# First stage of a fused conditional-mix, state-space and table-FFN kernel: how code bits are cut out of words, the order of its loads and expert network, and where dt is transposed

## The chip, the cores and the metric

The kernel runs on one core of a Trainium2 chip. A core has TensorE (PE: products, and transposes by an identity, into PSUM), VectorE (DVE), ScalarE (ACT), GpSimd (POOL) and SyncE (SP), which here only issues DMAs. Each engine works through a queue of its own in order and waits on semaphores. The metric is device time in microseconds, lower is better.

## The reference

Cut to what matters here (x is 128 x 32 x 512, `cond_128` is 128 x 128):

```python
h = gelu(cond @ W0 + b0); h = gelu(h @ W1 + b1)
att = softmax(h @ W2 + b2)                      # 8 experts
agg_w = einsum('bk,koi->boi', att, weight)      # one 32x32 mix matrix per batch
hidden = einsum('boi,bih->boh', agg_w, x) + (att @ bias_k)[:, :, None]
proj = hidden @ in_proj_w.T                     # gate, conv channels, and dt: the last 64 columns
dt_p = softplus(dt + dt_bias)
x = x + attention_like_scan(proj, dt_p, ...)    # second stage of the kernel
y = conv(x) + (cond @ c_weight.T)[:, :, None] + bias
# dequantisation: bit p of a weight's code is a bit of int32 plane p, 32 positions a word
idx = sum(((qweight[p][:, :, None] >> arange(32)) & 1) << p)   # p < 4 or p < 8
w_low, w_high = lut4[o, idx4], lut8[o, idx8]
out = x + where(norm(y) > 64, y @ w_high.T, y @ w_low.T) + bias
```

## The kernel before, in words

The program has three stages, one behind the other; a block ends when all engines are through it. The change touches the first, `stage1`; it ends at about 182 of 3663 us. The second (projections, convolution, scan) takes nearly all of the rest.

`stage1` first loads 14 small tensors from SP, and TensorE waits for all of them. The expert network is a chain over TensorE, ScalarE and VectorE (L276 to L293, L342 to L348, L401 to L427) to `agg`, the mix matrices. SP writes `agg`, `aggb` and `ctxb` to memory and reads them back as block-diagonal `mix` and `aggb_row` (L203 to L211). Then comes a loop over eight blocks of 512 tokens, in pairs (u is 0 or 1). For a block, TensorE makes four chunks of the hidden state (`mix_chunk`, eight matrix passes and one bias product each), ScalarE copies a chunk's high part (L372), VectorE subtracts it for the low part (`low_part`, L474), SP stores both (`h_d`, 2 MB) and loads the next x. `dt_block` (L316) makes dt, ScalarE and VectorE make its softplus (L359 to L363, L455, L458). GpSimd copies x by phases (`xp`, L270).

VectorE also does the work of the third stage's weights. `take_bits` (L391) cuts the bits of 8 planes out of `qw`: a byte of a word, shifted by s % 8 and masked by 1, for 32 bit positions and two halves of planes, so 64 instructions of 128x256 bytes; 28 stand ahead of the logits (L409) and 36 behind `att_t` (L417). L435 to L440 make `mask0` and the high code. Inside the loop `pair` (L465) and `join` (L470) build low-bit weights from `mask0`, `low_bits` and `lut4`. Behind the loop dt is transposed for all eight blocks (L336) and copied to `dt_all` (L509), by two PSUM banks that `dt_block` used.

## Time and profile before

| | before |
|---|---|
| median of 3 runs (lowest, highest) | 3664.96 us (3662.59, 3664.98) |
| profiled execution: its time, its span | 3664.37 us, 3662.6 us |
| TensorE, VectorE, ScalarE, GpSimd busy in the span | 3521.4, 3122.5, 1453.2, 469.3 us |
| mean granted TensorE clock | 0.988 |
| first product over the tokens starts | 70.28 us |
| last VectorE instruction of the first stage ends | 182.20 us |

The span is from the first to the last instruction of the profiled execution; 1.8 us of its time lie around it. Rows of the timeline give a start, a length, and in brackets how long the engine was idle before it and what released it.

### The profile page before, as it was taken

To read this page: it belongs to the slowest core of one execution; us is meant where nothing else is said; L and a number is where in the kernel's file an instruction comes from. 1 tells how busy PE (TensorE), PEld (TensorE's weight loads), DVE (VectorE), ACT (ScalarE), POOL (GpSimd) and SP (SyncE) were. 2 spreads that over 40 slices of the span, in tenths; PEclk is the share of its full clock that TensorE was granted. 3 is DMA by queue.
4 is the path that set the end of the run, shared out by engine and by line. 5 is a ranking of instruction groups with operands and counts; after the bars stand their busy time and mean duration, and the time that the engine had idled before them with its cause. 6 is when DMAs were issued, how large, how long until landed. Compare 5 with 4: busy or idle time off the path is not lost. (4 is left out here: it accounts for less than half of the span.)

```text
span 3662.6 us, 58842 instructions
## 1 busy us (share of the span) xinstructions
PE 3521.4 (96%) x19789; PEld 2880.3 (79%) x19789; DVE 3122.5 (85%) x4932; ACT 1453.2 (40%) x2215; POOL 469.3 (13%) x297
## 2 busy tenths in 40 slices
PE   3779999999999999999999999999999999998999
PEld 2568888888888888888888888888888888886888
DVE  7769999999999999999999999999999999997343
ACT  1534444444444444444444444444444444443111
POOL 2200011111000111110011111001111110010333
PEclk9889999999999999999999999999999999998999
DMA  3733335333533244323632353234333353334331
GB/s 95 309 127 114 126 115 183 126 126 116 178 135 126 103 161 160 126 109 115 206 112 105 126 206 117 110 123 177 132 115 126 129 186 115 126 111 128 102 96 55
DMA packets 220670, 490.26 MB, mean 134 GB/s; under 512 B 39594, under 2 KB 85066, under 8 KB 211042
## 3 DMA queue, kind: packets, MB, share of 16 engines
q1 hardware_dynamic: 217060, 489.10, 38.0%
q0 software_dynamic: 304, 0.82, 0.1%
q10 hardware_dynamic: 3280, 0.04, 0.1%
q8 instruction: 11, 0.18, 0.0%
q14 instruction: 15, 0.12, 0.0%
HBM read 320.51 MB, written 169.39 MB: 134 GB/s over the span
## 5 line engine op out<-in xcount | busy, mean ns | idle before, releaser
L743 PE MATMUL bank<-ht,wt 128*128 128x512 f32 x7680 | 1862.9, 397 | 7.3 <-DMA ht<-h_d 7.3
L743 PEld LDWEIGHTS bank<-ht,wt 128*128 128x128 f32 x7680 | 1427.2, 188 | 352.8 <-issue 18.5
L965 DVE SCALAR_TENSOR_TENSOR xc<-bank,cvw,xc 128x496 f32<-128x496 f32 (+2 forms) x1152 | 821.0, 717 | 95.9 <-ACT xc L880 45.4
L880 ACT ACTIVATE xc<-bank,cvb,cvw 128x512 f32<-128x512 f32 x384 | 299.3, 779 | 1126.7 <-PE bank L743 1126.7
L838 PE MATMUL bank<-wot,gy 128*128 128x512 f32 x3072 | 737.5, 396 | 0.0
L838 PEld LDWEIGHTS bank<-wot,gy 128*128 128x128 f32 x3072 | 567.3, 188 | 127.5 <-issue 11.0
L719 POOL TENSOR_TENSOR r<-rv,neg_half 128x4 f32<-128x4 f32 x64 | 89.7, 1402 | 2490.5 <-DVE rv L1053 2490.5
L987 DVE TENSOR_TENSOR m<-cbm,y 128x1024 f32<-128x1024 f32 x256 | 301.5, 1220 | 7.8
L716 POOL TENSOR_TENSOR segr<-adts,mask_le 128x1024 fp32r<-128x1024 f32 x128 | 242.7, 1917 | 381.5 <-DVE adts L956 381.5
L870 ACT ACTIVATE gy<-z 128x512 fp32r<-128x512 f32 x256 | 162.0, 633 | 320.5 <-DVE z L1027 320.5
L866 ACT ACTIVATE z<-bank 128x512 f32<-128x512 f32 x256 | 150.6, 588 | 278.9 <-PE bank L743 278.9
L760 PE MATMUL bank<-m,dtx 128*64 128x128 f32 x4096 | 251.8, 276 | 0.0
L760 PEld LDWEIGHTS bank<-m,dtx 128*64 128x64 f32 x4096 | 220.9, 137 | 34.2 <-issue 34.2
L862 ACT ACTIVATE xc<-xc 128x512 f32<-128x512 f32 x384 | 233.2, 623 | 14.4 <-DVE xc L965 13.7
L1023 DVE SCALAR_TENSOR_TENSOR y<-xc,dsk,bank 128x512 f32<-128x512 f32 x256 | 190.1, 743 | 47.3 <-PE bank L760 47.3
L1027 DVE SCALAR_TENSOR_TENSOR z<-z,nw,y 128x512 f32<-128x512 f32 x256 | 192.3, 751 | 26.6
L1265 PE MATMUL p_y<-wq,x3t 128*128 128x512 f32 x768 | 189.1, 402 | 0.0
L994 DVE TENSOR_TENSOR dtx<-bank,dt_all 128x512 f32<-128x512 f32 x256 | 168.0, 689 | 21.6 <-PE bank L750 17.5
L1016 DVE TENSOR_TENSOR gy<-z,gy 128x512 fp32r<-128x512 f32 x256 | 175.4, 685 | 0.0
L1065 DVE SCALAR_TENSOR_TENSOR acc<-bank,r,acc 128x512 f32<-128x512 f32 x256 | 173.7, 742 | 0.0
L1265 PEld LDWEIGHTS p_y<-wq,x3t 128*128 128x128 f32 x768 | 143.4, 190 | 32.6
L933 DVE TENSOR_SCALAR leaf<-mask,lut 128x512 int32<-128x512 int32 x320 | 166.9, 538 | 0.0
(162 smaller groups left out, 3088.5 us busy)
## 6 DMA issues: line engine op xcount, KB each, us to landing
ht<-h_d SPq DMA_DIRECT2D x64, 2048.0 KB, 7.8
acc<-acc_d SPq DMA_DIRECT2D x64, 1024.0 KB, 7.2
wt_d<-wnext SPq DMA_DIRECT2D x128, 512.0 KB, 3.1
acc_d<-acc SPq DMA_DIRECT2D x64, 1024.0 KB, 4.3
wt<-wt_d SPq DMA_DIRECT2D x70, 512.0 KB, 8.2
stage<-in_L_attn_in_proj_w SPq DMA_DIRECT2D x106, 256.0 KB, 2.7
h_d<-ht_out SPq DMA_DIRECT2D x8, 2048.0 KB, 7.2
wot<-wt_d SPq DMA_DIRECT2D x28, 512.0 KB, 6.2
```

The costliest lines, as they stand in the source:

```text
L716: pool.tensor_tensor(segr[:, half, :, :], adts[:, half, :].bitcast(F32).unsqueeze(2).to_broadcast([P, TT * HG, L]), sh.mask_le[:, :].unsqu ...
L743: ins = pe.matmul(pb[:, :], wt[:, n, l, k, :], ht[:, rr, k, :], start=(q == 0 and k == 0), stop=(q == 2 and k == KC - 1))
L760: ins = pe.matmul(bank[YB[c % 2]][u * HP:(u + 1) * HP, t * P:(t + 1) * P], dtx[:, t, h * HP:(h + 1) * HP], m[:, h, t, :], start=True, stop ...
L838: ins = pe.matmul(bank[OUT[t]][:, :], gy[:, c, l, t * P:(t + 1) * P], wot[:, rr, c, :], start=(c == 0 and q == 0), stop=(c == CT - 1 and q ...
L862: act.activation(xc[:, n, :], xc[:, n, :], ACT.Silu).then_inc(s_silu, 1)
L880: act.activation(xc[:, n, :], bank[PROJ_BANK[n]][:, :], ACT.Identity, bias=cvb[:, n:n + 1], scale=cvw[:, n, TAPS - 1:TAPS]).then_inc(s_tap, 1)
L965: ins = dve.scalar_tensor_tensor(dst, src, cvw[:, n, TAPS - 1 - k:TAPS - k], dst, ALU.mult, ALU.add)
L987: dve.tensor_tensor(m[:, :, t, :].rearrange("p h (c l) -> p h c l", l=L), cbm[:, t, :].rearrange("p (c l) -> p c l", l=L).unsqueeze(1).to_ ...
L1016: dve.tensor_tensor(gy[:, c, 1, :], z[:, c, :], gy[:, c, 0, :].bitcast(F32), ALU.subtract).then_inc(s_ulo, 1)
L1023: dve.scalar_tensor_tensor(y[:, c, :], xc[:, 2 + c, :], dsk[:, c:c + 1], bank[YB[c % 2]][:, :], ALU.mult, ALU.add).then_inc(s_y, 1)
L1027: dve.scalar_tensor_tensor(z[:, c, :], z[:, c, :], nw[:, c:c + 1], y[:, c, :], ALU.mult, ALU.mult).then_inc(s_u, 1)
L1265: ins = pe.matmul(p_y[t % 2][q][:, :], x3t[:, l, t, r, :], wq[:, q, rr, r, :], start=(n == 0 and r == 0), stop=(n == 2 and r == R - 1))
```

## The change

Four edits, all in `stage1`:

- **Bits.** `bits` is [128, 8 planes, 4, 512] bytes. One instruction shifts whole int32 words of `qw` by s (0 to 7) and masks them by 0x01010101, so that each of the four bytes of a result is one bit of one plane. There are 8 instructions of 128x512 words, each writing every eighth word. The bytes then lie in another order than the positions. Three ScalarE copies of 2048 bytes put planes 1 to 3 in order (`low_bits`), the `mask0` instruction does it for plane 0 as it reads, and a ScalarE copy behind the loop does it for the high code. The high code is joined by shifts and ORs of words, in six instructions behind the loop. All bit work stands behind the expert network.
- **Loads.** Six small loads come from SP, ahead of x; four needed ones and four later ones come from ScalarE's queue. TensorE waits for the first ten only. GpSimd makes the identity first and issues the loads of `qw` and the tables after `mix` is cleared.
- **Expert network.** The transposes of `wdt` and their copies move to its end, so ScalarE's first function is Gelu. The side product goes to `p_h[0]`.
- **dt.** `turn_dt` transposes block 2jj-2 and 2jj-1 in the next pair's loop round, into the banks `p_mlp` and `p_wdt`, which the loop left unused; `keep_dt` copies on VectorE. Two blocks are left for the end. TensorE's loop is written out.

```diff
+        def by_position(plane):
+
+            return plane.rearrange("p t (w s k) -> p t w k s", s=8, k=4)
...
+                for dst, src in ((cond[:, :], a["cond_128"]), (w0[:, :], a["L0_cond_W0"]),
+                                 (b0[:, :], a["L0_cond_b0"].rearrange("(p o) -> p o", o=1)),
+                                 (w1[:, :], a["L0_cond_W1"]),
+                                 (b1[:, :], a["L0_cond_b1"].rearrange("(p o) -> p o", o=1)),
+                                 (w2[:, :], a["L0_cond_W2"])):
                     sp.dma_start(dst, src).then_inc(s_ld, 16)
-                sh.n_small = 16 * len(small)
...
-                pe.wait_ge(s_ld, sh.n_small)
-                pe.wait_ge(s_const, 4)
+                pe.wait_ge(s_ld, 16 * NLD)
+                pe.wait_ge(s_const, 2)
                 pe.transpose(p_mlp[:, 0:NB], cond[:, :], sh.ident[:, :])
                 pe.transpose(p_mlp[:, NB:NB + L], cw[:, :], sh.ident[0:L, 0:L]).then_inc(s_pe, 1)
+                pe.wait_ge(s_dve, 2)
+                pe.matmul(p_mlp[:, 256:256 + NB], w0[:, :], cond_t[:, :], start=True, stop=True).then_inc(s_pe, 1)
+                pe.matmul(p_h[0][:, 0:L], cond_t[:, :], cw_t[:, :], start=True, stop=True).then_inc(s_pe, 1)
+                pe.wait_ge(s_act, 1)
+                pe.matmul(p_mlp[:, 384:384 + NB], w1[:, :], h1[:, :], start=True, stop=True).then_inc(s_pe, 1)
+                pe.wait_ge(s_act, 2)
+                pe.matmul(p_mlp[:, 192:192 + NEXP], h2[:, :], w2[:, :], start=True, stop=True).then_inc(s_pe, 1)
...
+                pe.wait_ge(s_ld2, 16 * NLD2)
...
                 pe.wait_ge(s_mix, 16 * (BT + 1))
-                with pe.Fori(0, NBLK // 2) as jj:
+                pe.wait_ge(s_dve, 11)
+
+                def turn_dt(j, u):
+                    pe.wait_ge(s_dtsp, j + 2)
+                    pe.wait_ge(s_dt, j + 1)
+                    for t in range(TT):
+                        ins = pe.transpose(p_dtT[u][:, t * H:(t + 1) * H], dt_t[:, ds(j * BLK + t * P, P)], sh.ident[0:H, 0:H])
+                    ins.then_inc(s_dtT, 1)
+
+                def pair_of_blocks(jj, first):
...
                     dt_block(0)
+                    if not first:
+                        turn_dt(2 * jj - 2, 0)
                     mix_chunk(1, 2)
                     mix_chunk(1, 3)
                     dt_block(1)
...
-                pe.wait_ge(s_dtpos, NBLK + 2)
-                for j in range(NBLK):
-                    pe.wait_ge(s_dtsp, j + 2)
...
+                    if not first:
+                        turn_dt(2 * jj - 1, 1)
+
+                pair_of_blocks(0, True)
+                for jj in range(1, NBLK // 2):
+                    pair_of_blocks(jj, False)
+                turn_dt(NBLK - 2, 0)
+                turn_dt(NBLK - 1, 1)
...
+                for dst, src in ((cw[:, :], a["L0_cond2_c_weight"]), (b2[:, :], a["L0_cond_b2"].partition_broadcast(NB)),
...
+                                 (bias_k[:, :], a["L0_cond_bias_k"])):
+                    act.dma_start(dst, src).then_inc(s_ld, 16)
+                for dst, src in ((side[:, :], a["fside_S_0"].partition_broadcast(NB)),
...
+                                 (alog[:, :], a["L0_attn_A_log"].partition_broadcast(P))):
+                    act.dma_start(dst, src).then_inc(s_ld2, 16)
                 act.wait_ge(s_pe, 2)
+                act.activation(h1[:, :], p_mlp[:, 256:256 + NB], ACT.Gelu, bias=b0[:, :]).then_inc(s_act, 1)
+                act.wait_ge(s_pe, 4)
+                act.activation(h2[:, :], p_mlp[:, 384:384 + NB], ACT.Gelu, bias=b1[:, :]).then_inc(s_act, 1)
+                act.wait_ge(s_dve, 4)
+                act.activation(att[:, :], logit[:, :], ACT.Exp, bias=nmax[:, :], accum_out=esum[:, :]).then_inc(s_act, 1)
+                act.wait_ge(s_pe, 8)
...
+                act.wait_ge(s_bits, 1)
+                for b in (1, 2, 3):
+                    act.activation(sh.low_bits[:, b, :, :].rearrange("p t (w k s) -> p t w k s", s=8, k=4), by_position(bits[:, b, :, :]),
+                                   ACT.Copy).then_inc(s_plane, 1)
                 high_pair(0, True)
                 with act.Fori(1, NBLK // 2) as jj:
                     high_pair(jj, False)
                 softplus_log(NBLK - 1, 1)
+                act.wait_ge(s_bits, 6)
+                act.activation(sh.hi[:, :, :].rearrange("p t (w k s) -> p t w k s", s=8, k=4), by_position(bits[:, 4, :, :]),
+                               ACT.Copy).then_inc(s_plane, 1)
...
-                def take_bits(first, last):
-
-                    for half, planes in enumerate((sh.low_bits, high_bits)):
-                        for s in range(first, last):
-                            ins = dve.tensor_scalar(planes[:, :, :, :].rearrange("p n t (w s) -> p n t w s", s=32)[:, :, :, :, s],
-                                                    qbyte[:, 4 * half:4 * half + 4, :, :, s // 8], s % 8, 1,
-                                                    ALU.logical_shift_right, ALU.bitwise_and)
+                bit_words = bits[:, :, :, :].rearrange("p n t i -> p (n t i)").bitcast(I32)
+                WORDS = OT * DM // 4
+
+                def take_bits():
+
+                    v = bit_words.rearrange("p (n t w s) -> p n t w s", n=8, t=OT, s=8)
+                    for s in range(8):
+                        ins = dve.tensor_scalar(v[:, :, :, :, s], qw[:, :, :, :].rearrange("p t n w -> p n t w"), s,
+                                                byte_ones[:, :].bitcast(I32), ALU.logical_shift_right, ALU.bitwise_and)
                     ins.then_inc(s_bits, 1)
...
-                dve.wait_ge(s_q, 16 * (OT + 2))
-                take_bits(0, 14)
+                dve.wait_ge(s_pe, 5)
+                dve.tensor_tensor(logit[:, :], p_mlp[:, 192:192 + NEXP], b2[:, :], ALU.add).then_inc(s_dve, 1)
...
-                dve.tensor_scalar(att[:, :], att[:, :], erec[:, :], None, ALU.mult).then_inc(s_dve, 1)
+                dve.tensor_copy(att_t[:, :], p_agg[0][0:NEXP, 0:NB]).then_inc(s_dve, 1)
+                dve.wait_ge(s_ld2, 16 * NLD2)
                 dve.wait_ge(s_pe, 7)
-                dve.tensor_copy(att_t[:, :], p_agg[0][0:NEXP, 0:NB]).then_inc(s_dve, 1)
-                take_bits(14, 32)
-                dve.wait_ge(s_pe, 8)
...
+                dve.wait_ge(s_act, 4)
+                dve.tensor_tensor(wdt_t[:, 1, :, :].rearrange("p k h -> p (k h)"), p_wdt[:, 0:KC * H],
+                                  wdt_t[:, 0, :, :].rearrange("p k h -> p (k h)").bitcast(F32), ALU.subtract).then_inc(s_dve, 1)
...
+                dve.wait_ge(s_q, 16 * (OT + 2))
...
-                dve.tensor_scalar(sh.mask0[:, :, :], sh.low_bits[:, 0, :, :], -1.0, None, ALU.mult).then_inc(s_bits, 1)
-                dve.scalar_tensor_tensor(hi_sum[:, :, :], high_bits[:, 1, :, :], 2.0, high_bits[:, 0, :, :],
-                                         ALU.mult, ALU.add).then_inc(s_bits, 1)
-                for b in (2, 3):
-                    dve.wait_ge(s_bits, 2 + b)
-                    dve.scalar_tensor_tensor((hi_sum if b == 2 else sh.hi)[:, :, :], high_bits[:, b, :, :], float(1 << b), hi_sum[:, :, :],
-                                             ALU.mult, ALU.add).then_inc(s_bits, 1)
-
-                dve.wait_ge(s_const, 15)
+                dve.wait_ge(s_const, 16)
+                take_bits()
+                dve.wait_ge(s_bits, 1)
+                dve.tensor_scalar(sh.mask0[:, :, :].rearrange("p t (w k s) -> p t w k s", s=8, k=4), by_position(bits[:, 0, :, :]), -1.0, None,
+                                  ALU.mult).then_inc(s_bits, 1)
+
...
+                    for b in (5, 6, 7):
+                        plane = bit_words[:, b * WORDS:(b + 1) * WORDS]
+                        ins = dve.tensor_scalar(plane, plane, b - 4, None, ALU.logical_shift_left)
+                    ins.then_inc(s_bits, 1)
+                    dve.wait_ge(s_bits, 4)
+                    for b in (4, 6):
+                        plane = bit_words[:, b * WORDS:(b + 1) * WORDS]
+                        ins = dve.tensor_tensor(plane, plane, bit_words[:, (b + 1) * WORDS:(b + 2) * WORDS], ALU.bitwise_or)
+                    ins.then_inc(s_bits, 1)
+                    dve.wait_ge(s_bits, 5)
+                    plane = bit_words[:, 4 * WORDS:5 * WORDS]
+                    dve.tensor_tensor(plane, plane, bit_words[:, 6 * WORDS:7 * WORDS], ALU.bitwise_or).then_inc(s_bits, 1)
...
-                dve.wait_ge(s_bits, 7)
+                dve.wait_ge(s_bits, 3)
                 dve.wait_ge(s_lutx, 2)
+                dve.wait_ge(s_plane, 3)
+
+                def keep_dt(j):
+                    dve.wait_ge(s_dtT, j + 1)
+                    dve.tensor_copy(sh.dt[:, TT * j:TT * (j + 1), :].rearrange("p t h -> p (t h)"), p_dtT[j % 2][:, 0:TT * H]).then_inc(s_dt, 1)
...
                     low_part(0, 0)
+                    if jj > 1:
+                        keep_dt(2 * jj - 3)
...
                     low_part(1, 2)
+                    if jj:
+                        keep_dt(2 * jj - 2)
...
+                join_high_bits()
+                keep_dt(NBLK - 3)
                 softplus(NBLK - 1, 1)
-                for j in range(NBLK):
-                    dve.wait_ge(s_dtT, j + 1)
-                    dve.tensor_copy(sh.dt[:, TT * j:TT * (j + 1), :].rearrange("p t h -> p (t h)"), p_dt[j % 2][:, 0:TT * H]).then_inc(s_dt, 1)
+                keep_dt(NBLK - 2)
+                keep_dt(NBLK - 1)
```

### What stands in the queues

VectorE, from its first copy to the write-back of `agg`, before (L391 is `take_bits`, L409 to L417 the softmax):

```order
L401 COPY cond_t<-p_mlp 128x128
L402 COPY cw_t<-p_mlp 128x32
L404 TENSOR_TENSOR wdt_t<-p_wdt,wdt_t 128x256
L391 TENSOR_SCALAR low_bits<-qw 128x256 x14
L391 TENSOR_SCALAR high_bits<-qw 128x256 x14
L409 TENSOR_TENSOR logit<-p_mlp,b 128x8
L411 TENSOR_REDUCE nmax<-logit 128x1
L413 RECIPROCAL erec<-esum 128x1
L415 TENSOR_SCALAR att<-att,erec 128x8
L417 COPY att_t<-p_agg 8x128
L391 TENSOR_SCALAR low_bits<-qw 128x256 x18
L391 TENSOR_SCALAR high_bits<-qw 128x256 x18
```

and after, from `att_t` on (L420 is `take_bits`; the five instructions of the softmax stand right behind the first two copies):

```order
L440 COPY att_t<-p_agg 8x128
L445 COPY agg<-p_agg 128x16x32 x2
L447 CAST aggb<-p_mlp 128x32
L448 TENSOR_TENSOR ctxb<-p_h,side 128x32
L450 TENSOR_TENSOR aggb<-p_mlp,aggb 128x32
L452 TENSOR_TENSOR wdt_t<-p_wdt,wdt_t 128x256
L455 TENSOR_SCALAR alog<-alog 128x64
L459 TENSOR_TENSOR lut<-lut 128x32
L459 TENSOR_TENSOR lut<-lut 128x512
L420 TENSOR_SCALAR bits<-qw,byte_ones 128x512 x8
```

The 64 bit instructions are gone from between the first copies, the softmax and `agg`; eight now stand behind the tables.

VectorE, the end of the first stage, before (L455 and L458 are the softplus of a block, L509 the copies of dt):

```order
L458 TENSOR_TENSOR dt_t<-dt_t,sp_e 64x512
L470 COPY_PREDICATED w<-low_bits,leaf_0 128x512
L455 TENSOR_SCALAR dt_t<-p_dt,dtb 64x512
L458 TENSOR_TENSOR dt_t<-dt_t,sp_e 64x512
L509 COPY dt_all<-p_dt 128x256 x8
L164 UNCONDITIONAL_BRANCH
```

and after (L470 to L479 join the high code, L497 and L500 are the softplus, L491 is `keep_dt`):

```order
L500 TENSOR_TENSOR dt_t<-dt_t,sp_e 64x512
L512 COPY_PREDICATED w<-low_bits,leaf_0 128x512
L470 TENSOR_SCALAR bits<-bits 128x512 x3
L475 TENSOR_TENSOR bits<-bits 128x512 x2
L479 TENSOR_TENSOR bits<-bits 128x512
L491 COPY dt_all<-p_wdt 128x256
L497 TENSOR_SCALAR dt_t<-p_dt,dtb 64x512
L500 TENSOR_TENSOR dt_t<-dt_t,sp_e 64x512
L491 COPY dt_all<-p_mlp 128x256
L491 COPY dt_all<-p_wdt 128x256
```

Six joining instructions and one copy stand ahead of the last softplus, two copies behind it; the other five copies are in the loop.

TensorE, second half of a loop round, after (L314 and L317 are a chunk, L327 is `dt_block`, L304 `turn_dt`; in before, the same rows stand without L304, and L336 with 32 transposes behind the loop):

```order
L327 MATMUL p_dt<-ht_out,wdt_t 64x512 x12
L304 MATMUL p_mlp<-ident,dt_t 128x64 x4
L314 MATMUL p_agg<-mix,xb 128x128 x4
L317 MATMUL p_agg<-aggb_row,ones_row 128x512
L314 MATMUL p_agg<-mix,xb 128x128 x4
L317 MATMUL p_agg<-aggb_row,ones_row 128x512
L327 MATMUL p_dt<-ht_out,wdt_t 64x512 x12
L304 MATMUL p_wdt<-ident,dt_t 128x64 x4
L314 MATMUL p_h<-mix,xb 128x128 x4
```

Four transposes follow each `dt_block` from the second round on.

## Rows read from the trace of the kernel before

**Rows 1.** Windows: busy us by engine (instructions), granted clock, DMA share, GB/s.

```profile
38.00:61.00 23.00, 4.42 (x7) 1.91 (x7) 22.13 (x43) 0.54 (x3) 0.00 (x0) 1.00 0.00 0
...
120.00:150.00 30.00, 24.06 (x108) 15.65 (x108) 21.66 (x31) 13.33 (x18) 11.23 (x3) 0.78 0.89 355
```

**Rows 2.** Timeline: start us, us, engine, line, what [idle before, releaser].

```profile
0.81 1.28 ACT L342 ACT_TABLE_LOAD   x1 [0.81 <-PEq L1443]
...
3.64 0.43 SPq L181 DMA_DIRECT2D w<-in_L_cond_W  x1
...
7.00 0.59 SPq L181 DMA_DIRECT2D alog<-in_L_attn_A_log  x1
...
12.88 0.47 PE L276 MATMUL p_mlp<-ident,cond 128*128 128x128 f32 x1 [12.88 <-DMA alog<-in_L_attn_A_log]
...
13.63 0.20 POOL L265 MEMSET ones<- 128x128 f32 x1
```

**Rows 3.** Timeline: the expert network up to its logits.

```profile
14.58 0.77 PE L283 MATMUL p_mlp<-cond_t,w 128*128 128x128 f32 x2
14.64 1.28 ACT L344 ACT_TABLE_LOAD   x1
...
15.00 14.70 DVE L391 TENSOR_SCALAR low_bits<-qw 128x256 uint8<-128x256 uint8 x14
15.55 8.24 POOL L270 COPY xp<-xb 128x2048 f32<-128x2048 f32 x2 [1.72 <-DMA xb<-in_x]
15.94 0.37 ACT L344 ACTIVATE h<-p_mlp,b 128x128 f32<-128x128 f32 x1
...
17.62 0.59 PE L287 MATMUL p_mlp<-w,h 128*128 128x8 f32 x2 [0.46 <-ACT h L346]
```

**Rows 4.** Timeline: from the logits to the first product over the tokens.

```profile
37.00 0.69 DVE L409 TENSOR_TENSOR logit<-p_mlp,b 128x8 f32<-128x8 f32 x1
...
38.56 0.23 DVE L415 TENSOR_SCALAR att<-att,erec 128x8 f32<-128x8 f32 x1
...
39.47 10.12 DVE L391 TENSOR_SCALAR low_bits<-qw 128x256 uint8<-128x256 uint8 x18
...
43.17 0.47 PE L293 MATMUL p_mlp<-bias_k,att_t 8*128 8x32 f32 x2
...
58.73 2.26 DVE L422 COPY agg<-p_agg 128x512 f32<-128x512 f32 x2
...
61.27 0.34 SPq L203 DMA_DIRECT2D agg_d<-agg  x1
...
70.28 2.07 PE L303 MATMUL p_h<-mix,xb 128*128 x8 [26.63 <-DMA aggb_row<-aggb_d]
```

**Rows 5.** DMA issues of the next stage's start, from ScalarE's queue: KB each, us to landing.

```profile
cvb<-in_L_attn_conv_bias ACTq DMA_DIRECT2D x2, 0.5 KB, 3.0
```

**Rows 6.** Timeline: VectorE, one leaf instruction of the loop.

```profile
74.98 0.54 DVE L465 TENSOR_SCALAR leaf<-mask,lut 128x512 int32<-128x512 int32 x1
```

**Rows 7.** Groups by shape, ScalarE, 0 to 185 us: busy us, mean ns.

```profile
L372 ACT ACTIVATE ht_out<-p_h 128x512 fp32r<-128x512 f32 x16 | 9.2, 591 | 38.3 <-PE p_h L306 38.2
...
L350 ACT ACTIVATE mask_gtr<-mask_gt 128x128 fp32r<-128x128 f32 x1 | 0.3, 294 | 0.0
```

**Rows 8.** Timeline: inside the loop over blocks.

```profile
112.72 3.51 DVE L465 TENSOR_SCALAR leaf<-mask,lut 128x512 int32<-128x512 int32 x1
...
119.76 4.86 PE L316 MATMUL p_dt<-ht_out,wdt_t 128*64 128x512 f32 x12 [4.97 <-DVE ht_out L474]
```

**Rows 9.** Timeline: the end of the first stage.

```profile
175.10 0.34 SPq L229 DMA_DIRECT2D w_d<-w  x1
...
176.96 0.68 DVE L458 TENSOR_TENSOR dt_t<-dt_t,sp_e 64x512 f32<-64x512 f32 x1 [3.14 <-ACT sp_e L363]
...
181.35 0.85 DVE L509 COPY dt_all<-p_dt 128x256 f32<-128x256 f32 x2 [0.42 <-PE p_dt L336]
```

**Rows 10.** Waits of SyncE's queue, 150 to 185 us: us in total, times, longest us.

```profile
SPq L164 <- DMA w_d<-w: 3.5, 1, 3.5
```

More of the change, by code:

```diff
@@ L70 @@
 PREP = 8
+NLD, NLD2 = 10, 4
 PROJ_BANK = (0, 1, 2, 0, 1, 2, 0, 1, 2, 0)
@@ L233, in _ @@
             def _(pool):
+                pool.memset(sh.ident[:, :], 0.0).then_inc(s_const, 1)
+                pool.wait_ge(s_const, 1)
+                pool.affine_select(out=sh.ident[:, :], in_=sh.ident[:, :], compare_op=ALU.not_equal, fill=1.0,
+                                   base=0, pattern=[[-1, P]], channel_multiplier=1).then_inc(s_const, 1)
+                pool.memset(ones_row[:, :].bitcast(F32), 1.0).then_inc(s_const, 1)
+                pool.memset(mix[:, :, :], 0.0).then_inc(s_const, 1)
                 q_v = a["L0_ffn_qweight"].rearrange("n (t p) w -> t p n w", p=P)
@@ L265, in _ @@
                 pool.memset(sh.ones[:, :], 1.0).then_inc(s_const, 1)
+                pool.memset(byte_ones[:, :], 1).then_inc(s_const, 1)
                 for jj in range(NBLK // 2):
@@ L273, in _ @@
             def _(pe):
-                pe.wait_ge(s_ld, sh.n_small)
-                pe.wait_ge(s_const, 4)
+                pe.wait_ge(s_ld, 16 * NLD)
+                pe.wait_ge(s_const, 2)
                 pe.transpose(p_mlp[:, 0:NB], cond[:, :], sh.ident[:, :])
                 pe.transpose(p_mlp[:, NB:NB + L], cw[:, :], sh.ident[0:L, 0:L]).then_inc(s_pe, 1)
+                pe.wait_ge(s_dve, 2)
[5 more added lines that the diff above has]
+                pe.matmul(p_mlp[:, 192:192 + NEXP], h2[:, :], w2[:, :], start=True, stop=True).then_inc(s_pe, 1)
+                pe.wait_ge(s_dve, 6)
+                pe.transpose(p_agg[0][0:NEXP, 0:NB], att[:, :], sh.ident[:, :]).then_inc(s_pe, 1)
+                pe.wait_ge(s_dve, 7)
+                for u in range(2):
+                    pe.matmul(p_agg[u][:, :], att_t[:, :], experts[:, u * 512:(u + 1) * 512], start=True, stop=True)
+                pe.matmul(p_mlp[:, 208:208 + L], att_t[:, :], bias_k[:, :], start=True, stop=True).then_inc(s_pe, 1)
+                pe.wait_ge(s_ld2, 16 * NLD2)
                 for k in range(KC):
@@ L329, in _ @@
                     dt_block(1)
-                pe.wait_ge(s_dtpos, NBLK + 2)
-                for j in range(NBLK):
-                    pe.wait_ge(s_dtsp, j + 2)
-                    pe.wait_ge(s_dt, j + 1)
-                    for t in range(TT):
-                        ins = pe.transpose(p_dt[j % 2][:, t * H:(t + 1) * H], dt_t[:, j * BLK + t * P:j * BLK + (t + 1) * P], sh.ident[0:H, 0:H])
-                    ins.then_inc(s_dtT, 1)
+                    if not first:
+                        turn_dt(2 * jj - 1, 1)
@@ L345, in _ @@
-                act.wait_ge(s_pe, 5)
-                act.activation(h2[:, :], p_mlp[:, 384:384 + NB], ACT.Gelu, bias=b1[:, :]).then_inc(s_act, 1)
-                act.wait_ge(s_dve, 5)
-                act.activation(att[:, :], logit[:, :], ACT.Exp, bias=nmax[:, :], accum_out=esum[:, :]).then_inc(s_act, 1)
+                for dst, src in ((cw[:, :], a["L0_cond2_c_weight"]), (b2[:, :], a["L0_cond_b2"].partition_broadcast(NB)),
+                                 (experts[:, :], a["L0_cond_weight"].rearrange("k o i u -> k (o i u)")),
+                                 (bias_k[:, :], a["L0_cond_bias_k"])):
+                    act.dma_start(dst, src).then_inc(s_ld, 16)
```

69 lines of the change are left out of this document (17 added, 52 removed).

## Prediction, made before the changed kernel ran

> **What bounds the kernel now.** The table of times gives 3664.4 us for the profiled execution, 0.6 below the median of the three runs shown; all sums below are made against 3664.4. TensorE is busy 96% of the span, but the change lies in the first stage, so I read windows there. From 38 to 61 us VectorE is busy 22.1 of 23 us, TensorE 4.4, ScalarE 0.5, and nothing is moved [rows 1]. From 120 to 150 us no engine is full, but the DMA share is 0.89 at 355 GB/s [rows 1]: the loop lives near its transfers. So the stage has three parts: a start that waits for loads, a middle that waits for VectorE's bits, and a loop.
>
> The start: TensorE's first transpose begins at 12.88, released by `alog`, the last of 14 loads, issued at 7.00 to 7.59 [rows 2]. The middle: the product for the logits starts at 17.62 [rows 3], yet VectorE adds the bias at 37.00 [rows 4], because 28 bit instructions stand in its queue. The last expert product ends at 43.17 + 0.47 = 43.64; the copies of `agg` start at 58.73 [rows 4], behind 36 more. SP writes `agg` at 61.27, and the first product over the tokens starts at 70.28, 9.0 us later, by the DMA `aggb_row` [rows 4]. This is one chain, and everything in the stage is behind its last link.
>
> **The change part by part.** Call S the start of the first transpose in the new kernel.
>
> *Loads.* Seven issues from SP end at 3.64 + 0.43 = 4.07 [rows 2], so six end near 3.6; ScalarE, free at 0.81 [rows 2], issues its four needed ones by about 2.7. From issue to landing I have two bounds: 3.0 us for a small load of ScalarE's queue on a quiet chip [rows 5], and 12.88 - 7.59 = 5.3 us for the last one here, which runs beside the large tables [rows 2]. S is 6.6 or 8.9. The tables now come later and only x follows, so I take S = 7.0, near the quiet row, an estimate.
>
> The Trainium skill (DMA: Bandwidth & Descriptors, Issuing engines are not separate DMA queues) says that issuing from several engines saves only the issue time. By that rule the second queue is worth its four issues, some 1.9 us of the 5.9 that I give to the start, and the rest must come from waiting for fewer loads.
>
> *Expert network.* S to the logit product was 17.62 - 12.88 = 4.74. Gelu began at 15.94, held by a table load from 14.64, though its product ended at 14.58 + 0.77 = 15.35 [rows 3]: 0.6 that goes. The side product now stands behind that product and not ahead of it, for which I take 0.4, half of the 0.77 row. About 1.0 less, so the product runs from S + 3.7 to S + 4.3. From logits to the last expert product it is 43.64 - 37.00 = 6.6, from the copies of `agg` to SP's write 61.27 - 58.73 = 2.5 [rows 4]. The write is at S + 13.5 (with 0.1 for a wait), the first product over tokens 9.0 later, at S + 22.5 = 29.5. Before: 70.28. **This is -40.8 us.**
>
> *Bits, now behind the network.* From 20.5 on VectorE has the rest of `wdt` (0.4), `alog` and the tables (1.1), which may sit behind GpSimd's copies until 22.1 (below): the bits start at 23.2. An instruction is 512 words. Low bound: 0.54, a leaf of the same size [rows 6]. High bound: twice the old instruction of 256 elements, 10.12 / 18 = 0.56 [rows 4], so 1.12, if what costs is each scattered write. I take 0.8, between: 8 x 0.8 = 6.4, to 29.6 (27.5 to 32.2). Then three ScalarE copies: 128 elements take 294 ns and 512 take 591 [rows 7], so 0.77 ns an element, 2048 take 1.78, three 5.3, to 34.9. High: four times the 512 row each, 2.36, to 39.3. The cover is TensorE's first four chunks, which need no result of VectorE: each has 2.07 us of passes [rows 4] and a bias product, so it lasts until at least 29.5 + 8.3 = 37.8. `mask0` (1.2) runs beside ScalarE. Cost 0; at the high bounds 1.5. The 43 us of bit work before and the three sums behind it (2.3 each) are thus gone from VectorE's way, but only what lay on the chain above counts.
>
> *dt in the loop.* TensorE gets 4 transposes for six blocks, VectorE five copies of 0.42 (two are 0.85 [rows 9]); a set of transposes is about what VectorE waits there, 0.42 [rows 9]. Where nothing hides them: 5 x 0.42 + 6 x 0.42 = 4.6. They are hidden by TensorE's wait before a `dt_block` (4.97 us [rows 8]) and by the transfers (0.89). I take +1.0, mostly for the set ahead of the next pair's first chunk. Below nothing: a leaf took 3.51 us beside a copy of GpSimd [rows 8]; a shift in time may miss one of these, -3. The queued waits are met in order: `turn_dt` comes before the chunk whose part `keep_dt` stands behind, so `keep_dt` finds its data. If not, `low_part`, the h store and `dt_block` are queued behind it.
>
> *End.* The last softplus ends near 177.6 and eight copies follow to 181.35 + 0.85 = 182.2 [rows 9]. Now two follow, with one set of transposes beside the first: 178.5. The six joins (6 x 0.54 = 3.2) and one copy (0.4) stand ahead of the last softplus's first half, and VectorE waited 3.1 us for ScalarE between its halves [rows 9]; at worst 0.5 sticks out. But SP's last wait, for `w_d`, issued at 175.10 to 175.44, lasts 3.5 [rows 9, 10], to 178.9; ScalarE's copy of the high code from 176.9 takes 1.8, to 178.7. **-3.3 us** (bounds -2 and -3.7).
>
> Sum: -40.8 + 0 + 1.0 - 3.3 = -43.1, and 3664.4 - 43.1 = 3621.3. The other stages are unchanged and start earlier.
>
> **The rivals.**
>
> *GpSimd's copy catches the softmax.* GpSimd does the same work as before plus a small memset, so its first x copy can start at about 13.63 + 0.20 + 0.1 = 13.9, if x is there. The two copies take 8.24 [rows 3], until 18.0 and 22.1. Before, 14 bit instructions beside them took 14.70, where 14 x 0.56 = 7.9 were due [rows 3, 4]: VectorE stood still for about 6.8 us. The scaling of `att` (the row at 38.56 [rows 4]) lies at S + 5.9 = 12.9. If S is 8.0 or more it waits to 18.0, and from there to the products over tokens it is 70.28 - 38.56 less the 15.1 of bits, 16.6: 34.6, or 5.1 later. Time 3626.4. For it: S may be 8.9. Against: my S leaves 1.0.
>
> The Trainium skill (SBUF — State Buffer, Who interferes with whom) says that GpSimd and a VectorE copy or tensor_scalar in a two-port mode lock each other out for a whole instruction, whoever comes first. By that rule the row at 38.56 is one that can be caught; the trace agrees as far as the stalled bit instructions and the leaf of 3.51 go.
>
> *The bits are late.* If scattered words cost 1.12 and byte reads with a stride of four cost ScalarE twice 1.78, the planes are ready at 32.2 + 10.7 = 42.9, 5 past the cover: 3626. For it: old byte writes took 0.56 for 256. Against: fewer, wider writes.
>
> *The loop pays in full.* 4.6 instead of 1.0, with a GpSimd stall of 3.5 more: 3628. Against: the share of 0.89.
>
> *The start moves but the loop doesn't:* if x or the phase copies bound the first round, part of the gain waits there. The copies end at 22.1, before 29.5, so this needs a transfer that the trace doesn't show late; 10 us lost, 3631.
>
> *Slower.* `turn_dt` at a pair's end waits for the softplus of the block before on VectorE, and the next chunks are queued behind it. If that softplus came a whole pair late, each of three rounds would lose up to a quarter of 182.2 - 70.3, 28 us: 3621.3 + 84 = 3705. It decides from 43.1 / 3 = 14.4 us a round. Against: it stands ahead of the `low_part` that `dt_block` waits for anyway.
>
> **How the numbers follow.** My forecast 0.56 (its own range 3616 to 3626); softmax caught 0.16; bits late 0.08; loop in full 0.08; start given back 0.04; more gained (S near 6, a stall missed: 3616 and below) 0.06; slower 0.02. The range 3613 to 3631 leaves out the last two's far parts. What a measurement of this kernel tells from no change is about 0.2%, 7.3 us. Every case but two is beyond it: faster 0.96, within 0.02, slower 0.02.
>
> **What would show it.** The first chunk of TensorE near 29.5 (34.6 if caught, with an `att` row of some 4 us); the first transpose released by a load of S near 7; bit instructions at 0.5 to 1.1 us; ScalarE's plane copies ended before TensorE's fourth chunk; from the first chunk to the end of the last dt copy 109 to 111 us, where it was 182.2 - 70.3 = 111.9. The prediction is wrong if the loop grows by more than the start loses, or if the bits hold the first chunk's high part past 38.

## The result, and the profile after

| | before | after |
|---|---|---|
| time, median of 4 runs | 3664.97 us (3662.59 to 3666.22) | 3620.15 us (3618.3 to 3620.65) |
| span of the profiled execution | 3662.6 us | 3618.7 us |
| granted TensorE clock, mean | 0.988 | 0.990 |

The ratio is 0.9876 (95% interval 0.9864 to 0.9889): 1.2% faster. The prediction was 3621.3, 1.1 us above the median.

The page, engines (busy us, share of the span, instructions):

```profile
PE 3519.7 (97%) x19789; PEld 2875.8 (79%) x19789; DVE 3082.9 (85%) x4879; ACT 1459.2 (40%) x2218; POOL 468.5 (13%) x298
```

The timeline after, from the start to the first product over the tokens (start us, us, engine, line, what [idle before, releaser]). It answers to [rows 2 to 4]:

```profile
0.81 0.43 ACTq L357 DMA_DIRECT2D cw<-in_L_cond_c_weight  x1
2.37 0.29 ACTq L357 DMA_DIRECT2D bias_k<-in_L_cond_bias_k  x1
3.18 0.43 SPq L182 DMA_DIRECT2D w<-in_L_cond_W  x1
4.96 1.28 ACT L364 ACT_TABLE_LOAD   x1 [4.96 <-issue]
7.57 0.47 PE L277 MATMUL p_mlp<-ident,cond 128*128 128x128 f32 x1 [7.57 <-DMA w<-in_L_cond_W]
9.59 0.37 ACT L364 ACTIVATE h<-p_mlp,b 128x128 f32<-128x128 f32 x1 [3.34 <-PE p_mlp L280]
13.14 0.28 DVE L438 TENSOR_SCALAR att<-att,erec 128x8 f32<-128x8 f32 x1
13.34 3.81 POOL L271 COPY xp<-xb 128x2048 f32<-128x2048 f32 x1
18.38 1.96 DVE L445 COPY agg<-p_agg 128x512 f32<-128x512 f32 x2 [4.21 <-PE p_mlp L291]
20.62 0.34 SPq L203 DMA_DIRECT2D agg_d<-agg  x1
22.71 4.16 DVE L420 TENSOR_SCALAR bits<-qw,byte_ones 128x512 int32<-128x512 int32 x8
26.90 5.51 ACT L400 ACTIVATE low_bits<-bits 128x2048 uint8<-128x2048 uint8 x3 [4.53 <-DVE bits L420]
29.22 2.08 PE L314 MATMUL p_h<-mix,xb 128*128 128x128 f32 x8 [10.33 <-DMA aggb_row<-aggb_d]
33.02 0.69 DVE L516 TENSOR_TENSOR ht_out<-p_h,ht_out 128x512 fp32r<-128x512 f32 x1 [4.52 <-ACT ht_out L394]
40.13 2.08 PE L314 MATMUL p_h<-mix,xb 128*128 128x128 f32 x8
```

The releaser of the first product is the same as before, `aggb_row`, but the `agg` copies now wait for TensorE and not behind bits. The bits start 2.1 us behind the write of `agg_d`, and all planes are ready at 26.90 + 5.51 = 32.41, when TensorE is in its second chunk. The fifth chunk, the first that needs VectorE (it waits for the first low part, the row at 33.02), starts at 40.13.

Inside the loop, one round with dt's transposes and copy and a collision with a GpSimd copy (before: [rows 8]):

```profile
70.64 0.47 PE L304 MATMUL p_mlp<-ident,dt_t 64*128 64x64 f32 x4
71.07 3.87 POOL L271 COPY xp<-xb 128x2048 f32<-128x2048 f32 x1 [7.99 <-DMA xb<-in_x]
71.71 3.53 DVE L507 TENSOR_SCALAR leaf<-mask,lut 128x512 int32<-128x512 int32 x1
77.42 0.40 DVE L491 COPY dt_all<-p_mlp 128x256 f32<-128x256 f32 x1
79.08 0.69 PE L327 MATMUL p_dt<-ht_out,wdt_t 128*64 128x512 f32 x1 [4.96 <-DVE ht_out L516]
```

The transposes (0.47) and `keep_dt` (0.40) now lie ahead of a wait of TensorE that is as long as before (4.96, before 4.97).

The end of the stage, and the first load of the next one (before: [rows 9]):

```profile
131.67 0.72 DVE L512 COPY_PREDICATED w<-low_bits,leaf 128x512 f32<-128x512 uint8 x1
132.29 1.08 DVE L470 TENSOR_SCALAR bits<-bits 128x512 int32<-128x512 int32 x3
133.41 1.29 DVE L475 TENSOR_TENSOR bits<-bits 128x512 int32<-128x512 int32 x2
134.31 0.34 SPq L229 DMA_DIRECT2D w_d<-w  x1
134.73 0.69 DVE L479 TENSOR_TENSOR bits<-bits 128x512 int32<-128x512 int32 x1
136.77 1.89 ACT L407 ACTIVATE hi_code<-bits 128x2048 uint8<-128x2048 uint8 x1
136.89 0.68 DVE L500 TENSOR_TENSOR dt_t<-dt_t,sp_e 64x512 f32<-64x512 f32 x1 [0.48 <-ACT sp_e L385]
138.34 0.42 DVE L491 COPY dt_all<-p_wdt 128x256 f32<-128x256 f32 x1 [0.43 <-PE p_wdt L304]
140.11 1.30 SPq L743 DMA_DIRECT2D stage<-in_L_attn_in_proj_w  x3
```

Of the 3.14 us that VectorE stood still for ScalarE here [rows 9], 0.48 are left: the joins fill them. The same two landmarks before, the last join of `w` and the next stage's first load:

```profile
171.26 0.72 DVE L470 COPY_PREDICATED w<-low_bits,leaf 128x512 f32<-128x512 uint8 x1
184.02 15.21 SPq L696 DMA_DIRECT2D stage<-in_L_attn_in_proj_w  x10
```

Where the time went, by landmarks of both traces:

| us | before | after | change |
|---|---|---|---|
| first product over tokens starts | 70.28 | 29.22 | -41.06 |
| from there to the start of the last join of `w` | 100.98 | 102.45 | +1.47 |
| from there to the end of the last dt copy | 10.94 | 7.09 | -3.85 |
| from there to the next stage's first load | 1.82 | 1.35 | -0.47 |
| from there to the end of the span | 3478.6 | 3478.6 | 0 |

The sum is -43.9, the difference of the spans. Each column is one execution; how far such stretches differ between executions is shown below, with dt behind the loop.

### The profile page after: what moved, and what is told of

Its sections match the earlier page's. It is cut to its first block and busy times, and to the rows that moved or that the text cites. A ratio compares the mean times of both kernels' runs of the same rounds, so it can differ in the third digit from the quotient of the medians.

```text
span 3618.7 us, 58730 instructions
## 1 busy us (share of the span) xinstructions
PE 3519.7 (97%) x19789; PEld 2875.8 (79%) x19789; DVE 3082.9 (85%) x4879; ACT 1459.2 (40%) x2218; POOL 468.5 (13%) x298
## 5 line engine op out<-in xcount | busy, mean ns | idle before, releaser
L909 ACT ACTIVATE xc<-xc 128x512 f32<-128x512 f32 x384 | 233.1, 623 | 13.9 <-DVE xc L1012 13.2
```

Of the source, the lines that this page charges most:

```text
L909: act.activation(xc[:, n, :], xc[:, n, :], ACT.Silu).then_inc(s_silu, 1)
```

## The experiments

Each is the changed kernel with one edit, unless said otherwise. "Before" was run on the same chip each time, and gave 3661.6 to 3666.7. Where no interval is given, the kernel ran once and has one time.

**The old bits in their old place**, with the new loads, expert network and dt.

```diff
+                dve.wait_ge(s_q, 16 * (OT + 2))
+                take_bits(0, 14)
...
+                take_bits(14, 32)
...
-                take_bits()
```

> The changed kernel, but with the old bit extraction at its old places (28 instructions ahead of the logits, 36 behind att_t). Chain theory: the bits on VectorE's queue carry the gain, so the first chunk starts near 69 us in place of 29.2, and the time is 3660 to 3663 us; earlier loads and the reordered network alone are worth under 3 us. Rival, each part worth its own: the earlier first transpose (7.6 against 12.9 us) and the Gelu load still give 6 us, the first chunk near 64 us, time near 3657.

Measured: 3661.57 us, 2.0 below before (3663.61). The first transpose starts at 6.94, 5.9 earlier than before, and yet the logits come at 36.20 and the first product over tokens at 69.41:

```profile
18.02 11.21 DVE L414 TENSOR_SCALAR low_bits<-qw 128x256 uint8<-128x256 uint8 x14 [9.94 <-DMA lut<-in_L_ffn_lut]
36.20 0.86 DVE L429 TENSOR_TENSOR logit<-p_mlp,b 128x8 f32<-128x8 f32 x1
```

Both came as the chain reading had it. An early network is worth nothing while its logits stand behind bits that themselves wait for the tables.

**Only the new bits**, in the new place; loads, network and dt as before. The diff is against the changed kernel and cut to TensorE's first wait.

```diff
-                pe.wait_ge(s_ld, 16 * NLD)
-                pe.wait_ge(s_const, 2)
+                pe.wait_ge(s_ld, sh.n_small)
+                pe.wait_ge(s_const, 4)
```

> The kernel before with only the new bits, behind the network; loads, network order and dt as before. Chain theory: first transpose at 12.9 us, first chunk 21.7 + 1.0 later, at 35.6, or near 40 if the scaling of att meets GpSimd's second copy; with the old dt at the end (2.3 us) the time is 3629 to 3634. Rival, the earlier loads are the larger part: above 3640.

Measured: 3627.89, 35.7 below before and 1.1 below the range expected. The first transpose is at 12.93, released by `alog` as before:

```profile
35.84 2.07 PE L309 MATMUL p_h<-mix,xb 128*128 x8 [11.21 <-DMA aggb_row<-aggb_d]
```

The scaling of `att` came at 19.55, just where the first of GpSimd's two copies ended (15.91 + 7.54 / 2 = 19.7), and took 0.23: it was not caught. So the bits alone give 35.7, the rest alone 2.0, and both together 44.8 by medians: some 7 us of loads, network and dt count only once the bits are off the chain.

**The old bits behind the network.** All 64 old instructions and the three sums, in the new place.

```diff
-                take_bits()
+                take_bits(0, 32)
```

> The changed kernel with the 64 old bit instructions and three sums, but all behind the network. Chain theory: first chunk still at 29.2 us, then VectorE needs 64 x 0.54 + 8.1 = 43 us from 22.7, so the first low part comes near 65 us in place of 33.0 and the fifth chunk near 66 in place of 40.1: 26 us later, time 3646 to 3650. Rival, the place alone matters and the bits' own length is hidden: 3620 to 3625.

Measured: 3651.89, 31.7 above the changed kernel and 1.9 above the range expected. The first product over tokens is at 28.64, but VectorE reaches the first low part only in the last of these rows:

```profile
22.07 17.75 DVE L414 TENSOR_SCALAR low_bits<-qw 128x256 uint8<-128x256 uint8 x32
39.48 17.93 DVE L414 TENSOR_SCALAR high_bits<-qw 128x256 uint8<-128x256 uint8 x32
45.22 15.68 POOL L272 COPY xp<-xb 128x2048 f32<-128x2048 f32 x1 [23.83 <-DMA xb<-in_x]
57.44 4.54 DVE L458 TENSOR_SCALAR mask<-low_bits 128x2048 int32<-128x2048 uint8 x1
69.14 0.69 DVE L500 TENSOR_TENSOR ht_out<-p_h,ht_out 128x512 fp32r<-128x512 f32 x1
```

The new order, with the loads, the network and dt of the change, gives 12 of the 44.8 us; the cheaper instructions are needed for the rest. And a GpSimd copy of 3.8 us took 15.68 beside VectorE's instructions: it ended at 60.90, 3.5 behind the last of the 64 (39.48 + 17.93 = 57.41). The `mask0` instruction behind them took 4.54, where it is 1.23 in the changed kernel, until that copy was over: 3.3 of the 4.1 us by which the low part is later than the 65 expected.

**The new bits ahead of the network's logits.**

```diff
+                dve.wait_ge(s_const, 16)
+                dve.wait_ge(s_q, 16 * (OT + 2))
+                take_bits()
...
-                take_bits()
```

> The changed kernel with its eight bit instructions ahead of the logits. Chain theory: they wait for the tables' loads (15 us) and are caught by GpSimd's copies until 22 us, so they end at 24 to 26 us and the first chunk comes 17.3 us behind the logits, at 41 to 43 us: time 3632 to 3634. Rival, cheap bits do no harm anywhere: at most their own 4.2 us, 3624.

Measured: 3632.63, 12.5 above the changed kernel; the first product over tokens moves from 29.22 to 42.19, by 13.0. Two rows say why 4 us of work cost 13 (the first transpose is 0.6 earlier here, so from there on it is 13.6):

```profile
17.58 3.81 POOL L271 COPY xp<-xb 128x2048 f32<-128x2048 f32 x1 [0.44 <-DMA xb<-in_x]
17.96 7.39 DVE L420 TENSOR_SCALAR bits<-qw,byte_ones 128x512 int32<-128x512 int32 x8 [9.89 <-DMA lut<-in_L_ffn_lut]
```

VectorE stands for 9.89 us at the wait for the tables with the logits queued behind it. Their product ended at 11.24, so 6.7 of these count; then come the bits' own 4.16, and 7.39 - 4.16 = 3.2 us go to the copy that they collide with.

**TensorE waits for all fourteen loads.**

```diff
                 pe.wait_ge(s_ld, 16 * NLD)
+                pe.wait_ge(s_ld2, 16 * NLD2)
```

> The changed kernel, but TensorE waits for all fourteen loads before its first transpose. The last of the later four should land at 9.5 to 11 us, which moves the first transpose by 2 to 3.5 us. Lock theory: att then meets GpSimd's first copy and waits to 17.2, and the first chunk is at 33.3 us whatever the landing: time 3624. Rival, a plain shift: first chunk at 31.2 to 32.7, no long att row.

Measured: 3623.11 (3621.31 to 3627.43), ratio 0.9887 (0.9871 to 0.9904). The first transpose starts at 11.25, a little behind the range expected: the last of the fourteen, `alog`, landed 6.8 us after its issue at 4.34. The first product over tokens is at 32.98, 21.7 later. The run was also to show the softmax caught by GpSimd's copy, and hardly did:

```profile
13.35 3.80 POOL L271 COPY xp<-xb 128x2048 f32<-128x2048 f32 x1
16.81 0.37 DVE L438 TENSOR_SCALAR att<-att,erec 128x8 f32<-128x8 f32 x1
```

The scaling of `att` came 0.3 us before the copy's end and lost 0.1. The run shows the shift of the loads only.

**The softmax in the middle of a copy.** As the last, and four small memsets ahead of GpSimd's copies.

```diff
+                for n in range(4):
+                    pool.memset(spare[:, :], 0.0).then_inc(s_const, 1)
+                    pool.wait_ge(s_const, 17 + n)
```

> The kernel in which TensorE waits for all fourteen loads, with four GpSimd memsets of 512 elements (some 2.1 us) more ahead of its first x copy. There the scaling of att came at 16.81 and the copy ended at 17.15; now the copy should run from 15.5 to 19.3, with att in its middle. Lock theory: the att row is 2.5 us long, ends at 19.3, and the first chunk comes near 35.2 in place of 32.98. Rival, an instruction of eight elements is not caught: row of 0.3 us, first chunk 21.7 us behind the first transpose, 33.0.

Measured: 3626.01. Now the collision is there:

```profile
15.68 7.56 POOL L275 COPY xp<-xb 128x2048 f32<-128x2048 f32 x2
17.81 1.70 DVE L442 TENSOR_SCALAR att<-att,erec 128x8 f32<-128x8 f32 x1
```

An instruction that takes 0.23 to 0.37 us elsewhere took 1.70, from 17.81 to 19.51, until the first of two copies ended (15.68 + 7.56 / 2 = 19.5). From the first transpose (12.25) to the first product over tokens (35.32) it is 23.1, where it was 21.7 without the collision: the 1.4 that it lost stand on the chain.

**GpSimd's copies earlier**, four small instructions of GpSimd moved behind the first two.

```diff
+                    if jj == 1:
+                        pool.memset(sh.neg_half[:, :], -0.5).then_inc(s_const, 1)
```

> The changed kernel, with four small GpSimd instructions (iota, three memsets, some 0.4 us) behind its first two x copies, so that the first copy can start near 12.9 us, ahead of the scaling of att at 13.14. Lock theory: att is caught until the copy ends at 16.8, its row is near 4 us long and the first chunk comes 3.6 us later: time 3624. Rival, so small an instruction is not caught, or x isn't there before 13.2: no change, 3620.

Measured: 3619.56 (3617.34 to 3620.75), ratio 0.9876 (0.986 to 0.9893), as the changed kernel. It missed: the copy started at 13.04, but in this run the loads landed early (first transpose 6.76) and `att` was scaled at 12.35, ahead of it.

**ScalarE copies the phases of x**, so that no GpSimd copy runs in the stage.

```diff
+                        act.activation(xp[u][:, :, :, :], xb[u][:, :, :].rearrange("p t (m r) -> p t r m", r=R), ACT.Copy).then_inc(s_xp, 1)
```

> The changed kernel with the x copies by phases on ScalarE (2048 elements, 1.9 us) in place of GpSimd, ahead of each block's high parts. Lock theory: the leaf instructions, 870 ns in the mean beside GpSimd, fall to 540, and no instruction of VectorE is over 1.3 us. Transfers-bound loop: the time gains 0 to 2 us only, 3618 to 3620. Rival, VectorE's stalls set the loop's pace: 8 to 10 us less, 3611.

Measured: 3621.63 (3621.2 to 3622.38), ratio 0.9882 (0.9866 to 0.9899). Groups of the loop by shape, busy us and mean ns; first this kernel:

```profile
L387 ACT ACTIVATE xp<-xb 128x2048 f32<-128x2048 f32 x8 | 31.3, 3908 | 0.0
L505 DVE TENSOR_SCALAR leaf<-mask,lut 128x512 int32<-128x512 int32 x28 | 14.8, 539 | 0.1
```

and the changed kernel:

```profile
L507 DVE TENSOR_SCALAR leaf<-mask,lut 128x512 int32<-128x512 int32 x28 | 24.0, 870 | 0.1
```

The leaves' stalls, 9.2 us in sum, are gone, as expected, but the time is 1.5 above the changed kernel's and 1.6 above the range expected. The next stage's first load is at 142.12, 2.0 later than in the changed kernel, not earlier. By itself the run leaves two readings: VectorE's stalls don't set the loop's pace, or they do and ScalarE's 31.3 us took as much back. The first has one more thing for it. The leaves take 24.0 us in the changed kernel and 20.8 to 21.5 in the six kernels that have the new bits and the same loop, and the loop of these (next table) is 0.8 to 2.3 us longer, not shorter. That TensorE's waits and the transfers cover the stalls is argued and not shown.

**dt behind the loop**, as before, with the rest of the change.

```diff
-                turn_dt(NBLK - 2, 0)
-                turn_dt(NBLK - 1, 1)
+                for j in range(NBLK):
+                    turn_dt(j, j % 2)
```

> The changed kernel with all dt transposes and copies behind the loop, as before, in the new banks. By the two traces the loop took 1.5 us longer with dt inside and the end 3.9 us less: without it 3622.5 us. Rival, the loop hides dt wholly and its 1.5 us come from elsewhere: 3624. Rival, dt costs the loop what it saves at the end: 3620.

Measured: 3619.05 (3618.49 to 3619.18), ratio 0.9875 (0.9858 to 0.9891), 3.45 below the 3622.5 expected and nearest the rival that dt costs the loop what it saves at the end. The first product over tokens is at 28.61:

```profile
129.06 0.72 DVE L508 COPY_PREDICATED w<-low_bits,leaf 128x512 f32<-128x512 uint8 x1
139.58 0.42 DVE L487 COPY dt_all<-p_wdt 128x256 f32<-128x256 f32 x1
```

First product over tokens to last join is 100.45 (changed kernel 102.45), and from there to the last dt copy's end 10.94 (7.09). By these two traces dt in the loop costs 2.0 there and gives 3.85 behind it, 1.85 net. The other traces don't bear that out. Seven more kernels here turn dt in the loop and differ from the changed kernel in the work around it (the old bits in their old place, the new bits ahead of the logits, GpSimd's copies earlier, all fourteen loads, the softmax in a copy, one queue, the mix earlier); three besides this one turn it behind (before, only the new bits, the mix earlier with dt behind). One execution of each, us:

| | dt in the loop: changed kernel | the seven others | dt behind the loop, four kernels |
|---|---|---|---|
| first product over tokens to last join | 102.45 | 103.25 to 104.73 | 99.70 to 100.98 |
| from there to the end of the last dt copy | 7.09 | 7.00 to 8.15 | 10.94 to 11.78 |
| both | 109.54 | 110.73 to 111.73 | 111.39 to 111.92 |

So dt in the loop costs it 1.5 to 5 us and gives 3 to 5 behind it. Net, between the seven and the four, that is -0.3 to 1.2 us, and the changed kernel's profiled execution, with 109.54, is the one that stands out. The rest of the program, whose code is the same, took 3476.1 us in this execution and 3478.6 in the changed kernel's.

**All ten loads from SP's queue.**

```diff
+                    sp.dma_start(dst, src).then_inc(s_ld, 16)
...
-                    act.dma_start(dst, src).then_inc(s_ld, 16)
```

> The changed kernel with all ten needed loads on SP's queue, ahead of x (the four later ones stay on ScalarE's). Issue-time theory: four issues of 0.45 later, the first transpose at 8.6 to 9.0 us in place of 6.8 to 7.6, and the first chunk as much later, near 30.5. Rival, the two queues also overlap their landing: 10 us or more. Rival, the landing of other loads decides: no change.

Measured: 3618.24. The tenth load is issued at 5.09, 1.9 us later than the last of SP's six in the changed kernel (3.18), and the first transpose starts where it did, as in the rival that the landing of other loads decides:

```profile
5.09 0.29 SPq L187 DMA_DIRECT2D bias_k<-in_L_cond_bias_k  x1
7.54 0.48 PE L282 MATMUL p_mlp<-ident,cond 128*128 128x128 f32 x1 [7.54 <-DMA bias_k<-in_L_cond_bias_k]
```

In the kernels whose first transpose waits for the same ten loads from two queues it starts at 6.76 to 7.57. One run of this one at 7.54 puts the second queue's worth between 0 and 0.8 us.

**The mix earlier.** The product for the bias of `agg` goes ahead of the expert products, each `agg` copy waits for its own two products, SP writes `agg` with a semaphore of its own, and the four loads of `mix` go two to SP and two to ScalarE's queue, ahead of the write of `ctxb`.

```diff
+                load_mix(sp, 0)
...
+                load_mix(act, 2)
...
+                    dve.wait_ge(s_pe, 8 + u)
```

> The changed kernel with the bias product ahead of the two expert products, each half of agg copied as soon as its product is there, the write of agg not behind two other writes, the small row loaded first, and the four mix loads issued half by SP, half by ScalarE. Chain theory: 1.0 from the copies, 1.0 from the writes, 0.5 to 1.1 from the issues: the first chunk at 25.8 to 26.5 us for a first transpose at 7.0, where it was 28.6; time 3617.5, the bits still hidden (planes ready 5 us ahead of the fifth chunk). Rival, the bits and planes now hold the first low part beyond the fourth chunk: no gain.

Measured: 3616.34 (3615.18 to 3619.02), ratio 0.9873 (0.9856 to 0.9889).

```profile
7.16 0.47 PE L283 MATMUL p_mlp<-ident,cond 128*128 128x128 f32 x1 [7.16 <-DMA w<-in_L_cond_W]
19.22 0.33 SPq L213 DMA_DIRECT2D agg_d<-agg  x1
22.23 0.93 SPq L175 DMA_DIRECT2D mix<-agg_d  x2
26.64 2.08 PE L320 MATMUL p_h<-mix,xb 128*128 128x128 f32 x8 [7.93 <-DMA mix<-agg_d]
26.68 5.51 ACT L407 ACTIVATE low_bits<-bits 128x2048 uint8<-128x2048 uint8 x3 [3.06 <-DVE bits L427]
```

From first transpose to first product over tokens it is 19.5 and not 21.7. But the next stage's first load is at 139.51, only 0.6 earlier than in the changed kernel: against that trace, whose loop is the shortest of its kind, the gain is gone. Against the others it stands: from the first transpose to the next stage's first load it is 132.4 here, and 134.2 to 134.7 with GpSimd's copies earlier, with all fourteen loads and with one queue. So the edit is worth some 2 us in the stage; it is the lowest median of all kernels here, but that it is worth the 3.8 us between the medians is not shown.

**The mix earlier, with dt behind the loop.**

> The same, with the dt transposes behind the loop. By three traces dt inside costs the loop 2.0 us and saves 3.85 at the end: this should be 1.9 us slower than the run beside it, with a loop 2 us shorter. Rival, the loop's length depends on which VectorE instructions meet GpSimd's copies and not on dt: the loop is as long, and this 3.9 us slower, or the two are the same.

Measured: 3620.68 (3618.69 to 3624.27), ratio 0.9883 (0.9867 to 0.99). It is 4.3 above the last by medians, where 1.9 was expected, but its next stage starts its loads at 139.76, 0.25 later, after a first transpose 0.4 later (7.55). Its loop is 99.70 and that of the last 104.46, so dt has a part in the loop's length, against the rival; from the first product over tokens to the last dt copy's end it is 111.48 against 111.52. With the pair above (dt behind the loop 1.1 us lower) the two pairs of medians disagree, and the two pairs of traces give dt in the loop 1.85 and nothing. The sign of its worth stays open.

From the first transpose to the next stage's first load it is 132.2 here and 134.4 in the kernel with dt behind the loop: 2.1 for the earlier mix once more.

## Why the prediction was right, step by step

*The chain of the start* (S, S to first chunk). S was put at 7.0 and came at 7.57; over nine kernels that wait for the same ten loads from two queues it lies between 6.76 and 7.57, so 7.0 was inside the scatter. S to the first chunk was put at 22.5 and is 21.65: the logits came at S + 4.3 as forecast, and from logits to the last expert product (6.4, forecast 6.6), from copies to write (2.2, forecast 2.5) and from write to first chunk (8.6, forecast 9.0) each link was a little shorter. First chunk 29.5 forecast, 29.22 measured. The old bits in their old place (69.41) show that this is one chain through VectorE's queue.

*Why S came early.* Here a sentence of the prediction falls. It gave 1.9 of the 5.9 us to the second queue, by the rule of the Trainium skill (DMA: Bandwidth & Descriptors, Issuing engines are not separate DMA queues) that several engines save only issue time. One queue gave 7.54, so the second is worth 0.8 at most, by one run: issue time was not what was late. Waiting for fewer loads made most of the gain: waiting for all fourteen gives 11.25 with the same queues, 3.7 to 4.5 more than the nine kernels. What else lies between 11.25 and the 12.88 of before was not taken apart. The sum did not rest on that sentence.

*The bits.* Put at 0.8 us each, 6.4; measured 4.16 for eight, a share of 0.52 each, near the low bound. One row lasts 0.66, where a leaf's is 0.54, and two start 0.50 apart, where leaves start 0.45 apart: the instruction with its scattered words costs some 0.05 us more each, 0.4 in all, and not the doubling of the high bound. Plane copies 5.3 forecast, 5.51 measured. Ready at 32.4 instead of 34.9. The cost of 0 was right with 6.4 us of cover left: the first low part, which the fifth chunk waits for, ended at 33.02 + 0.69 = 33.71, and that chunk started at 40.13. The rival of late bits is out.

*dt in the loop.* This is the term that the prediction had too small. Forecast +1.0. The loop grew by 1.5 in the changed kernel's trace, but by 2.3 to 3.8 in the seven other kernels with the same loop. The mechanism fits, for the transposes for a pair's second block are ahead of the next pair's first chunk, as said, and the loop is shorter in all four kernels with dt behind it; how the cost is shared among transposes, copies and shifted collisions no run shows. Together with the end (+1.0 - 3.3 = -2.3 forecast up to the last dt copy) the changed kernel gives 109.54 - 111.92 = -2.4, the seven others -0.2 to -1.2. The prediction's sign, 109 to 111, holds for the changed kernel and for one of the seven. So that the two terms came out is luck of this one execution.

*The end.* Forecast -3.3 to the end of SP's wait; measured -3.85 to the last dt copy and -0.47 behind it, 4.3. The joins fitted in VectorE's wait for ScalarE without anything sticking out: after, they are followed by a wait of 0.48. I had taken 178.9 for the wait for `w_d` as the last event. After, the wait is again 3.5 but ends at 134.65 + 3.5 = 138.2, 0.6 before the last dt copy's end: the copies stayed last.

*The softmax rival, 0.16.* It did not occur, but the margin was 0.20 us from start to start: `att` started at 13.14 and the copy at 13.34. The prediction had 12.9 and 13.9, a margin of 1.0. GpSimd's start was mis-sized by 0.6: its memset of `ones` came at 13.15 and not at 13.63 as in [rows 2]. The mechanism is real (1.70 us in the run built for it), and it agrees with the Trainium skill (SBUF — State Buffer, Who interferes with whom), which says that whoever comes second is blocked for the other's whole instruction: the VectorE instruction waited for the end of one GpSimd copy, not of both. The price on a full catch, up to 3.8 us for one copy of that length, is an upper bound from the copy's row, since the run caught only 1.4 of it; the prediction's 5.1 had also counted S at 8.0.

*The sum.* -40.8 and 0 and +1.0 and -3.3 against -41.06, 0, +1.47 and -4.32: -43.1 forecast, -43.9 measured in the span. That it hit within 1.1 us is in part luck, twice over: the unchanged rest of the program takes 3474.8 to 3480.7 us in the executions profiled here and was equal in the two compared, and the changed kernel's loop was the shortest of its kind. What carries the result, -40.8 against -41.06 to the first product over tokens, doesn't hang on either.

## What to carry to other kernels

Look first for what stands in a queue ahead of a chain's small instructions: 4 us of bits ahead of a 0.2 us instruction cost the chain 13 us, since their own wait for data and their collision came with them, and behind the chain they cost nothing while TensorE had other chunks to do. Parts of such a change don't add: 35.7 and 2.0 alone, 44.8 together, because loads that come early are worth nothing until the queue behind them is free. Against an exclusive lock a margin of 0.2 us is luck and not design, and an edit worth under some 4 us here has to be read from the stage's landmarks in the trace, since the rest of the program scatters more than that. Even a landmark stretch needs several executions: the same loop differed by 2.3 us between eight kernels, and one pair of traces gave dt in the loop 1.85 us that the others don't.

## What the runs showed of the hardware that was not expected

- A VectorE shift-and-mask of 128x512 int32 words that writes every eighth word lasts 0.66 us and starts 0.50 behind the one before; a leaf of the same size with dense writes lasts 0.54 and starts 0.45 behind.
- ScalarE reads bytes with a stride of four at 1.90 us for 2048 elements (1898 ns mean), near what dense rows gave by extrapolation (1.78). Its f32 copy of the same 2048 elements with a stride takes 3.9 us, no less than GpSimd's 3.8 to 4.0.
- The collision works both ways: VectorE's leaf took 3.53 us beside a copy of 3.87, and a GpSimd copy took 15.68 beside VectorE's bit instructions, four times its own length, and ended only 3.5 behind the last of them.
- Copies of VectorE that read PSUM (`agg`, 0.98 each, and 0.94 in the kernel with only the new bits, where no copy ran; `att_t`, 0.28 with and without a copy) ran at nearly full speed while a GpSimd copy was running; what was caught works in SBUF alone: the scaling of `att` (1.70), leaves (3.53), and the capping of `alog`, 1.24 beside the second copy at the start and 0.18 where no copy ran.
